# A two-layer kernel with its prologue and last tile reordered, and filler matmuls on TensorE where the prologue waits

## The reference, cut to what matters

```
# layer 0
h   = gelu(cond @ W0 + b0); h = gelu(h @ W1 + b1)
att = softmax(h @ W2 + b2)                         # 128 samples x 8 modes
y   = (sum_k att_k * weight_k) @ x + att @ bias_k  # a 64 x 64 matrix for each sample
x   = x + y @ W_base.T + b_base + 2 * sum_e w_e(y) * ((y @ A_e.T) @ B_e)
# layer 1
y   = grouped_conv1d(x, 9 taps) + cond @ c_weight.T + bias
x   = x + y @ base_w.T + base_b + 2 * (top-2 of 8 experts, rank 16 each)
```

## Time and profile before

| what | value |
|---|---|
| median of 3 runs (lowest to highest) | 2189.41 us (2189.12 to 2191.34) |
| the profiled execution: its own time, and its span | 2188.57 us, 2186.8 us |
| TensorE busy | 2143.8 us (98% of the span) |
| VectorE, GpSimd, ScalarE busy | 1356.8, 856.8, 508.9 us |
| DMA | 256.34 MB, mean 117 GB/s |

### The profile page before, as it was taken

The page is one execution under the profiler, slowest core; times in us unless marked ns, Lnnn a source line. Parts: engine busy times, 40 slices in busy tenths (PEclk is TensorE's granted clock), DMA queues, the critical chain, the costliest instruction groups (busy, mean ns, idle before and its releaser), DMA issues.

```text
span 2186.8 us, 40976 instructions
## 1 busy us (share of the span) xinstructions
PE 2143.8 (98%) x12684; PEld 2099.0 (96%) x12684; DVE 1356.8 (62%) x3539; ACT 508.9 (23%) x1179; POOL 856.8 (39%) x1052
## 2 busy tenths in 40 slices
PE   4999999999999999999999999999999999999998
PEld 4899999999999999999999999999999999999998
DVE  6777777777777777777555554555555555555554
ACT  3222121121222212222322222222222222222221
POOL 5534444344343443444533333333333333333331
PEclk9999999999999999999999999999999999999999
DMA  5433433333334333343544333344333343333432
GB/s 171 133 106 90 110 100 102 108 90 109 101 100 110 90 107 103 94 111 95 170 132 137 130 118 123 123 131 135 119 121 126 128 136 121 118 128 123 137 126 77
DMA packets 163554, 256.34 MB, mean 117 GB/s; under 512 B 21072, under 2 KB 103376, under 8 KB 163536
## 3 DMA queue, kind: packets, MB, share of 16 engines
q1 hardware_dynamic: 163232, 255.55, 38.0%
q10 hardware_dynamic: 304, 0.56, 0.1%
HBM read 122.01 MB, written 100.73 MB: 102 GB/s over the span
## 4 chain that ended last, share of the span: by engine, by line
PE 95%; DMA 1%; DVE 1%; ACT 1%; issue 1%; POOL 0%; SPq 0%; DVEq 0%; ACTq 0%
PE psB L870 73%; PE psB L896 8%; PE psT L846 3%; PE psT L852 3%; PE psT L850 3%; PE psT L851 3%; PE psT L847 1%; PE psB L883 1%; DMA Xraw<-in_x 0%; DMA shifted<-mixbuf 0%; DMA stage<-in_l0w 0%; POOL Wlo L347 0%; DMA outb<-in_condw 0%; ACT Whi L474 0%; SPq L322 0%
## 5 line engine op out<-in xcount | busy, mean ns | idle before, releaser
L870 PE MATMUL psB<-Whi,Yhi 128*128 128x384 f32 (+2 forms) x3072 | 732.3, 346 | 7.4 <-issue 7.4
L870 PE MATMUL psB<-Wlo,Yhi 128*128 128x384 f32 (+2 forms) x3072 | 714.7, 341 | 0.0
L870 PE MATMUL psB<-Whi,Ylo 128*128 128x384 f32 (+2 forms) x3072 | 710.9, 340 | 0.0
L356 POOL TENSOR_TENSOR Xlo<-Xraw,Xhi 128x256 fp32r<-128x256 f32 x512 | 419.9, 853 | 728.1 <-ACT Xhi L432 728.1
L870 PEld LDWEIGHTS psB<-Wlo,Yhi 128*128 128x128 f32 x3072 | 560.5, 189 | 0.0
L870 PEld LDWEIGHTS psB<-Whi,Ylo 128*128 128x128 f32 x3072 | 559.8, 189 | 0.0
L870 PEld LDWEIGHTS psB<-Whi,Yhi 128*128 128x128 f32 x3072 | 526.6, 190 | 22.2 <-issue 7.8
L385 POOL TENSOR_TENSOR res<-res,bias 128x256 f32<-128x256 f32 x256 | 183.3, 748 | 439.4 <-DMA res<-x_scratch 439.4
L448 ACT CAST Yhi<-Y 128x512 fp32r<-128x512 f32 x256 | 159.3, 622 | 602.1 <-DVE Y L619 342.6
L375 POOL TENSOR_TENSOR res<-Xraw,bias 128x256 f32<-128x256 f32 x256 | 223.1, 906 | 114.8 <-DVE outb L655 114.8
L625 DVE TENSOR_TENSOR Ylo<-Y,Yhi 128x512 fp32r<-128x512 f32 x256 | 210.3, 822 | 47.3 <-ACT Yhi L448 47.3
(11 more groups left out here) (90 smaller groups left out, 1899.3 us busy)
## 6 DMA issues: line engine op xcount, KB each, us to landing
Xraw<-in_x SPq DMA_DIRECT2D x64, 512.0 KB, 3.4
x_scratch<-outb SPq DMA_DIRECT2D x64, 512.0 KB, 2.7
x_block_scratch<-outb SPq DMA_DIRECT2D x512, 64.0 KB, 2.0
Xraw<-x_block_scratch SPq DMA_DIRECT2D x64, 512.0 KB, 4.8
res<-x_scratch SPq DMA_DIRECT2D x64, 512.0 KB, 4.4
out<-outb SPq DMA_DIRECT2D x64, 512.0 KB, 3.0
shifted<-mixbuf SPq DMA_DIRECT2D x128, 224.0 KB, 2.5
row<-row_scratch SPq DMA_DIRECT2D x128, 64.0 KB, 4.4
```

The costliest lines, as they stand in the source:

```text
L356: last = pool.tensor_tensor(Xlo[:, piece], Xraw[:, par, piece], as_f32(Xhi[:, piece]), ALU.subtract)
L870: last = mm(psB[:, 3 * par + b, 0:cols], y, w[:, k, BANK0[b]:BANK0[b] + cols], start=(k == 0 and y is yh and w is Whi), stop=(k == KT - 1 ...
```

## The change

The prologue is put in another order.

- SyncE issues all loads of weights, of tile 1, of the bias and of `b0raw` at once, and only then the stores and loads of attention and bias rows.
- For tiles 0 and 1 the attention and the bias rows no longer go through DRAM: TensorE spreads them over the partitions with small matmuls by a broadcast column of the identity (`spread_att`, `row_banks`), and makes `arow` by a matmul with a block-diagonal `bias_diag`, which is filled by two small loads. VectorE copies the results. `mixing_matrix(0)` reads the attention from PSUM.
- ScalarE does the Exp before `high_x(0)`.
- The low halves of weight blocks 0, 1, 2 are made on GpSimd, in four pieces each, and those of 3 to 7 on VectorE. Before, the odd blocks were GpSimd's and the even ones VectorE's.
- The mix of tile 1 begins after block 3 of tile 0 and not after block 1. `Blo` of layer 0 is made in step 1. What loads and splits the low-rank and convolution weights of layer 1 moves from steps 0 and 1 to steps 1 to 3, and the first `l1w` loads from step 1 to step 3; the first four steps of layer 0 are written out.

The last tile goes bank by bank: first bank 2 for all blocks, then bank 0, then bank 1, with `turn` and `up` of tile 127 between the blocks of bank 1, and the first part of `emit` after bank 0.

`keep_busy` is new as well: fp32 matmuls of the identity by itself into columns of a PSUM bank that nobody reads, 4 while TensorE waits for the softmax, 5 before the first mix, 1 after each of the chunks 1 to 3 of it, and 2 more before the first base product.

```diff
-MIX_AFTER_FIRST = (1, 3, 4, 5)
+MIX_AFTER_FIRST = (3, 4, 5, 6)
+LOW_W = ((3, 4, 5, 6, 7), (0, 2, 4, 6))
+LOW_W_POOL = ((0, 1, 2), (1, 3, 5, 7))
+PEELED = (4, 2)
...
+        att_banks, att_turned_bank = (psB[:, 3, 0:MODES], psB[:, 0, 256:256 + MODES]), psB[0:2 * MODES, 4, 0:STEPS]
+        arow_bank, row_banks = psB[0:STEPS, 5, 0:P], (psB[:, 2, 0:P], psB[:, 1, 256:256 + P])
+        unread = psB[:, 5, 256:256 + P]
...
-            load_w(range(0, 1))
-            sp.wait_ge(dve_cond, 4)
+            load_w(range(0, 3))
+            sp.dma_start(bias[:, :], l0b.partition_broadcast(P)).then_inc(bias_in, 16)
+            load_w(range(3, 4))
+            sp.dma_start(Xraw[:, 1, 0:H], x[P:2 * P, :]).then_inc(x_loaded[1], 16)
+            load_w(range(4, KT))
+            sp.dma_start(b0raw, l0B).then_inc(b0_in, 16)
+            sp.wait_ge(dve_cond, 6)
             sp.dma_start(atts.rearrange("a s k -> s a k"), att).then_inc(cond_out, 16)
-            load_w(range(1, 2))
-            sp.wait_ge(cond_out, 16)
+            sp.wait_ge(dve_cond, 8)
+            sp.dma_start(rows[0], arow).then_inc(cond_out, 16)
+            sp.dma_start(rows[1], crow).then_inc(cond_out, 16)
+            sp.wait_ge(cond_out, 48)
             for a in range(2):
                 sp.dma_start(attb[a * C:(a + 1) * C, :, :].rearrange("p s k -> p (s k)"),
                              atts[a].rearrange("s k -> (s k)").partition_broadcast(C)).then_inc(att_in, 16)
-            sp.wait_ge(dve_cond, 6)
-            sp.dma_start(rows[0], arow).then_inc(cond_out, 16)
-            sp.dma_start(rows[1], crow).then_inc(cond_out, 16)
-            load_w(range(2, 3))
-            sp.wait_ge(cond_out, 48)
-            for par in range(2):
-                sp.dma_start(row[:, par, :], rows[0, par, :].partition_broadcast(P)).then_inc(row_loaded[par], 16)
-            load_w(range(3, 5))
-            sp.dma_start(Xraw[:, 1, 0:H], x[P:2 * P, :]).then_inc(x_loaded[1], 16)
-            load_w(range(5, KT))
-            sp.dma_start(b0raw, l0B).then_inc(b0_in, 16)
-            sp.dma_start(bias[:, :], l0b.partition_broadcast(P)).then_inc(bias_in, 16)
+            def conv_weights(rs):
+                for r in rs:
+                    to = craw[r * GC:(r + 1) * GC, :, :, :].rearrange("p g w (t o) -> p g w t o", o=GC)
...
-                if isinstance(j, int) and n in (1, STEPS - 2):
-                    if n > 1:
+                if isinstance(j, int) and n == 1:
+                    sp.wait_ge(w_hi, KT)
+                    sp.wait_ge(w_lo, len(LOW_W[0]))
+                    sp.wait_ge(w_loP, len(LOW_W_POOL[0]))
+                    sp.dma_start(b1raw, l1B).then_inc(l1s_in, 16)
+                    sp.wait_ge(conv_zero, 1)
+                    conv_weights(range(BR // 2))
+                if isinstance(j, int) and n == 2:
+                    conv_weights(range(BR // 2, BR))
+                if isinstance(j, int) and n in (3, STEPS - 2):
+                    if n > 3:
                         sp.wait_ge(s_hi, 3)
                         sp.wait_ge(s_loP, 2)
-                    for k in range(0, KT // 2) if n == 1 else range(KT // 2, KT):
+                    for k in range(0, KT // 2) if n == 3 else range(KT // 2, KT):
                         sp.dma_start(stage[:, k, 0:H + NAG[1]], l1w.rearrange("(p k) n -> p k n", p=P)[:, k, :])\
                             .then_inc(w_in[k], 16)
...
             def split_lo(k, layer):
                 pool.wait_ge(w_hi, KT * layer + k + 1)
                 w = H + NAG[layer]
-                pool.tensor_tensor(Wlo[:, k, 0:w], stage[:, k, 0:w], as_f32(Whi[:, k, 0:w]), ALU.subtract)\
-                    .then_inc(w_loP, 1)
+                pieces = PIECES if layer == 0 else 1
+                for i in range(pieces):
+                    piece = slice(i * w // pieces, (i + 1) * w // pieces)
+                    last = pool.tensor_tensor(Wlo[:, k, piece], stage[:, k, piece], as_f32(Whi[:, k, piece]),
+                                              ALU.subtract)
+                last.then_inc(w_loP, 1)
...
             low_x(0, 0, 0)
-            for k in range(1, KT // 2, 2):
+            for k in LOW_W_POOL[0]:
                 split_lo(k, 0)
             low_x(0, 1, 0)
-            for k in range(KT // 2 + 1, KT, 2):
-                split_lo(k, 0)
-            pool.wait_ge(bias_in, 16)
...
+            pool.wait_ge(bias_in, 16)
             residual(0, 0, 0)
+            pool.wait_ge(mm_cond, 10)
+            pool.wait_ge(cond_out, 48)
+            residual(0, 1, 0)
             def step(j, par, lay0, lay, lay1, lay2):
                 n = 2 * j + par
-                if isinstance(j, int) and n == 0:
...
-                    pool.memset(craw, 0.0).then_inc(conv_zero, 1)
...
                 if isinstance(j, int) and n == 1:
+                    pool.wait_ge(w_hi, KT)
+                    pool.wait_ge(w_lo, len(LOW_W[0]))
+                    pool.wait_ge(w_loP, len(LOW_W_POOL[0]))
+                    pool.memset(craw, 0.0).then_inc(conv_zero, 1)
+                if isinstance(j, int) and n == 3:
                     pool.wait_ge(s_hi, 2)
                     pool.tensor_tensor(Blo[:, 1, :], b1raw, as_f32(Bhi[:, 1, :]), ALU.subtract).then_inc(s_loP, 1)
...
-            high_x(0, 0, 0)
             act.wait_ge(dve_cond, 2)
             for a in range(2):
                 nc.scalar.activation(ex[:, a, :], lg[:, a, :], ACT.Exp, bias=nmx2[:, a:a + 1],
                                      accum_out=sum2[:, a:a + 1]).then_inc(act_cond, 1)
+            high_x(0, 0, 0)
             act.wait_ge(consts, 3)
             for k in range(2):
                 split_w(k, 0)
             high_m(0)
-            for k in range(2, KT // 2):
+            for k in range(2, 4):
                 split_w(k, 0)
             split_y(0, 0, 0, range(2))
             high_x(0, 1, 0)
+            split_w(4, 0)
             high_m(1)
-            for k in range(KT // 2, KT):
+            for k in range(5, KT):
                 split_w(k, 0)
             act.wait_ge(b0_in, 16)
             nc.scalar.copy(Bhi[:, 0, :], b0raw).then_inc(s_hi, 1)
...
-                if 0 in chunks:
-                    dve.wait_ge(row_loaded[par], 16 * (j + 1))
+                if 0 in chunks and isinstance(n, int) and n < 2:
+                    dve.wait_ge(row_copied, n + 1)
+                elif 0 in chunks:
+                    dve.wait_ge(row_loaded[par], 16 * j)
...
+                very_last = isinstance(j, int) and n == 2 * STEPS - 1
                 dve.wait_ge(up_done, n + 1)
                 dve.wait_ge(rest_added, n + 1)
...
                 for b, (r0, r1) in enumerate(EIGHTHS):
+                    if very_last and b == 1:
+                        dve.wait_ge(up_done, n + 2)
...
-            dve.wait_ge(act_cond, 4)
-            nc.vector.reciprocal(rec2, sum2).then_inc(dve_cond, 1)
-            dve.wait_ge(dve_cond, 3)
-            nc.vector.tensor_tensor(att, ex, bcast(rec2, 2, MODES), ALU.mult).then_inc(dve_cond, 1)
-            dve.wait_ge(dve_cond, 4)
-            for a in range(2):
-                last = nc.vector.tensor_tensor(aprod[:, a], mixbs, bcast(att[:, a, :], 2, C), ALU.mult)
-            last.then_inc(dve_cond, 1)
-            dve.wait_ge(dve_cond, 5)
-            for a in range(2):
-                nc.vector.tensor_reduce(arow[:, a * C:(a + 1) * C], aprod[:, a].rearrange("p k o -> p o k"),
-                                        AX.X, ALU.add)
             nc.vector.tensor_tensor(crow.rearrange("p (a o) -> p a o", a=2),
                                     psT[0:STEPS, 0, 0:P].rearrange("p (a o) -> p a o", a=2),
                                     bcast(cbs, 1, 2), ALU.add).then_inc(dve_cond, 1)
             nc.vector.tensor_scalar(nbthr, bthrs, -1.0, None, ALU.mult).then_inc(dve_cond, 1)
-            dve.wait_ge(att_in, 32)
+            dve.wait_ge(act_cond, 4)
+            nc.vector.reciprocal(rec2, sum2).then_inc(dve_cond, 1)
+            dve.wait_ge(dve_cond, 5)
+            nc.vector.tensor_tensor(att, ex, bcast(rec2, 2, MODES), ALU.mult).then_inc(dve_cond, 1)
             dve.wait_ge(mix_in, 32)
-            mixing_matrix(0)
+            dve.wait_ge(mm_cond, 5)
+            nc.vector.tensor_tensor(prod, mixT, bcast(att_banks[0], 2, C), ALU.mult).then_inc(prod_ready, 1)
+            dve.wait_ge(mm_cond, 6)
+            nc.vector.tensor_copy(att_turned, att_turned_bank).then_inc(dve_cond, 1)
+            dve.wait_ge(prod_ready, 1)
+            nc.vector.tensor_reduce(agg[:, :], prod.rearrange("p k o -> p o k"), AX.X, ALU.add).then_inc(agg_ready, 1)
+            dve.wait_ge(mm_cond, 8)
+            nc.vector.tensor_copy(arow, arow_bank).then_inc(dve_cond, 1)
+            nc.vector.tensor_copy(att1, att_banks[1]).then_inc(att_copied, 1)
             low_m(0)
-            split_w(0, 0)
-            evacuate_y(0, 0, 0, range(NC))
-            split_y(0, 0, 0, range(2))
+            for n in range(2):
+                dve.wait_ge(mm_cond, 9 + n)
```

(75 more changed lines are left out.)

72 lines of the change are left out of this document (35 added, 37 removed).

## The result

| | before | after |
|---|---|---|
| median, us (lowest to highest, runs) | 2189.62 (2188.53 to 2191.34, 6) | 2180.89 (2180.32 to 2182.72, 6) |
| ratio, 95% interval | 1 | 0.9959 [0.9947, 0.997] |
| profiled execution: span, us | 2186.8 | 2178.6 |
| TensorE busy, us | 2143.8 | 2148.7 |

The kernel is faster by 8.7 us, 0.41%. The forecast was 2172.5, 17 us faster, with a range of 2165 to 2180; the measured time lies 0.9 us outside it, on the slow side. The direction was right, the size half of it.

What follows compares the result with a forecast made beforehand. TensorE bounds the kernel, busy 2143.8 of 2186.8 us, its waits mostly in the first 90 us. 2188.57 - 11.4 + 0 - 5.5 = 2171.7; with 0.84 from profiled execution to median, 2172.5, range 2165 to 2180.

Steps and rivals of the forecast that it cites:

- The prologue up to the first mix: Start of kernel: first mix at about 17.0, first evacuation at 18.0 against 23.48, 5.5 us earlier.
- The weights' queue: Weight loads, all issued first: done near 23, block 3 landing at 15 when wanted; any attention store delay hidden.
- one of the forecast's own signs of being wrong: Weight loads at the start: the forecast is wrong if weights land after ScalarE wants them.
- Tiles 0 and 1: First two tiles, to chunk 2 of tile 2's mix: VectorE's fixed order sets the pace; gain 11.4 us, bounds 7 and 15.
- contention: VectorE held by GpSimd's pieces between first evacuation and the matrix of tile 2: 2.5 us.
- the forecast's undisturbed sum: VectorE's work from first evacuation to the matrix of tile 2, at undisturbed durations with three Yhi waits: 23.1 us.
- Steps 1 to 4: Early layer 0 steps: moved loads and splits cost 0 us net, bounds -2 and +3.
- the recurrence of before's stalls: Tile 4: tile 2's old evacuation wait, 2.13 us, and up wait, about 0.8, recur; if not, gain 3.
- The last tile: Tile 127, bank by bank: ends at 2178.1 against 2183.65, gain 5.5 us (4.5 to 5.8).
- the slow ones: Rivals: clock low in tile 0, or weights or attention late; 2176 to 2184, chance 0.20.

Runs made afterwards that it cites:

- the early loads: Changed kernel with the memset in step 0 and the b1 and all 16 convolution loads in step 1 ahead of the store: 2176.26 us.
- the pieces: Changed kernel with GpSimd's two subtractions splitting b1 and the convolution weights issued as four instructions each: 2183.18 us, ratio 0.997.

## Why the prediction missed

- **The prologue up to the first mix: right.** First mix at 17.57 (17.0), first evacuation at 18.70 (18.0), first base product at 22.12 (near 22). The conditioning weights land at 6.3 where it was 5.57, which accounts for the 0.7 us at the first evacuation. Inside, two misses cover each other. The mixing matrix was ready at 16.21, not 14.5: besides those 0.7 us the product waited for the mixing weights until 12.24, and L602 and L603 took 0.80 and 0.75. The fillers then held the mix by 1.4 us, where 17.0 less 14.5 is 2.5. That the first mix came so near is in part luck.
- **The weights' queue: right.** It stays full up to about 23 (DMA share 0.68 in 22 to 24, 0.04 in 24 to 26). Block 3 came 1.06 us after ScalarE wanted it (its cast starts at 16.79), one of the forecast's own signs of being wrong; ScalarE then idled 2.45 us before its next use at 20.41, so it cost nothing. The attention store, 4 KB issued at 11.23, lands 12.5 us later, at 23.7, with the last weight block, and nobody waits for it; the row stores behind it land up to 25.5. The Trainium skill ("DMA: Bandwidth & Descriptors", Queues, rings and completion order) says that one engine's ring is consumed in order; the trace agrees in that the small store waited behind the loads, though it landed before the load of `b0raw` (25.0), which was issued ahead of it.
- **Tiles 0 and 1: mechanism right, 1.4 us short.** 10.0 for 11.4. The term that was mis-sized is contention, taken as 2.5. From the first evacuation at 18.70 to the matrix of tile 2 at 45.69 it took 27.0 us, where the forecast's undisturbed sum was 23.1, so contention and all else was 3.9. The five weight splits alone took 1.47 to 2.14 us, median 2.03, where 1.37 was their undisturbed time: 2.9 us in all. With the 0.7 of the late start the matrix is 2.1 us late (43.6 forecast), and weigh, Blo and the chunk behind it gave 0.7 back, 4.9 us for 5.6. Tile 1 began at 43.30, not 40.5.
- **Steps 1 to 4, 0 us with bounds of -2 and +3: this is the step that failed.** It measured 6.3 us of loss. The forecast said of the queued load that it "lands about 14 us after the emit, where it is wanted: 0, bound 1 each". It does land 14 us after the emit (59.56 to 73.33). Where it is wanted is what it had wrong. It doesn't say from which tile it took that; tile 2 of before fits, where the cast began 14.9 us after the store (69.53 to 84.40), and that tile itself ran 2 us late by the wait of the earlier trace rows. In a tile without stall `up` comes 13.1 us after the store (75.81 to 88.92 with the early loads), here 15.45, so it is wanted 2.3 us earlier. That costs 2.34 us at tile 2 and, since the loop repeats with the second eight loads, 2.34 at tile 3. At tile 4 the forecast took the recurrence of before's stalls at their old price, 2.13 and 0.8. The waits came (2.61 and 0.42), but the step lost 5.08, part of it at the low clock behind the wait. The `l1w` loads were seen and booked at 0.8; alone they hold the step by 4.2. The kernel with all loads early and the splits in pieces, 2171.29, shows that these causes are most of the miss. It is 1.2 us below the forecast 2172.5, but it also lacks the stalls that the forecast let recur; without them the forecast's own figure is 3 us less, 2169.5, and against that it is 1.8 us late, 1.4 of it from tiles 0 and 1. In the profiled executions the miss is 16.9 - 8.2 = 8.7 us: 1.4 in tiles 0 and 1, 6.3 in tiles 2 to 4, and 1.1 at the change of layers (the last point below), less 0.1 that the last tile gave more.
- **The last tile: right.** 5.5 forecast; 5.6 in the traces (gain 2.56 after the layers change, 8.2 at the end), 5.8 alone on the kernel before.
- **Of the rivals**, the slow ones (2176 to 2184, 0.20) held the time, but not by their mechanism, so that is luck: the clock was not low in tile 0, the attention did not come late, and the one late weight block cost nothing. A late input load two tiles on was in none of them.
- **What stays open.** At the change of layers the gain falls from 3.98 us (turn at 1086.69 and 1082.71) to 2.56 (`up` at 1090.60 and 1088.04), with a granted clock of 0.83 in 1080 to 1090. The wait of 1.5 us for `hw` (L784) that stands there is in three more of the kernels' traces and absent in the others. Among these is the second trace of the changed kernel: there nothing is lost between the layers (2.39 at the turn, 2.40 at `up`), but 1.4 us more in tiles 3 and 4, and the end is 8.0 us earlier than before where it is 8.2 in the first. So what is lost there belongs to the execution and not to the kernel, and how the loss is split over tiles 3 and 4 and the change of layers varies by over 1 us from one execution to the next. What decides it stays open.

## What to carry to other kernels

When a change makes one stage earlier, the next bound is often an issue queue: follow each load back through the engine that issues it, and take the time at which it is wanted from an undisturbed tile, not from one that was late for another reason. Compare tile by tile where the gain goes. Where removing a stall gives nothing, look for a second of the same length behind it before dropping the edit: here the pieces were worth nothing twice and 2.2 us the third time. And a slow clock costs where TensorE sets the step (17.76 us for 16.13); inside a loop that a load sets, the time it loses is taken from a wait. So the price of a wait can include the slow stretch behind it: count the steps, not the wait.

## What the hardware showed that I had not expected

- Two waits of the same length in the same place had different consequences: after 2.18 us the granted clock read 0.66 over the next 5 us (1.2 GHz in the two middle ones), after 2.20 us in the kernel with pieces it read 1.00, and in before it stayed at 1.00 after the 2.13 us wait of the earlier trace rows. The wait of 2.24 us one tile on, in the kernel with pieces, was followed by 0.72 from 95 to 100. And after the wait of 1.9 to 2.3 us before tile 1, which all kernels with the new prologue have, the clock stayed at 1.00 in six traces and fell to 0.50 in five, for some 3 us in four of them and 6 in one; that one alone lost 1.9 us by it. What the chip goes by, these runs don't tell.
- At the start the granted clock reads 1.00 while matmuls take nearly twice their time: without fillers groups of three base products took 1.31, 1.17 and 1.17 us before they took 0.70, and the windows from 20 to 26 read 1.00. The durations show this, the clock column doesn't. With the fillers the slow pace ends near 18.3.
- A load of 512 KB that usually lands 3.3 us after its issue took 7.3 behind four loads of weights, and 7.45 in the kernel before.
- The prologue's fillers make no measurable difference, since VectorE sets the pace there: 2180.89 against 2181.45, and 2171.29 against 2170.62. The Trainium skill ("TensorE: Matmul & The Clock Gate", Why this matters for your kernels) advises to keep TensorE busy; the trace agrees as to the pace of the matmuls, and the medians show no gain in time.
